# Two of the four token tiles of each late layer norm go to VectorE, the statistics' small sums too, and the queues behind the head loop are written in a new order

## The reference, cut to what matters

```python
x = x + attn_a(layernorm(x), ...)   # 16 heads of 64, causal softmax, output weights Wo, bo
x = x + ffn(layernorm(x), ...)      # 128 -> 512 -> 128, relu
x = x + attn_b(layernorm(x), ...)   # one head of 128, causal, a slope over the distance
x = x + ffn(layernorm(x), ...)      # the same weights again

def _layernorm(x, axis=-1, eps=1e-05):
    m = jnp.mean(x, axis=axis, keepdims=True)
    v = jnp.var(x, axis=axis, keepdims=True)
    return (x - m) / jnp.sqrt(v + eps)
```

## Time and profile before

| | |
|---|---|
| Median of 3 runs | 575.68 us (575.47 to 575.82) |
| Profiled execution, its own time | 579.0 us |
| Span in that profile | 577.0 us |
| Busy in the span | PE 528.2 us, ACT 468.5, POOL 455.8, DVE 444.7 |
| Slots | to about 417 us |
| Work behind the slots | about 417 to 577 us |

### The profile page before, as it was taken

How to read it: one execution, slowest core, us unless ns; L and a number is a source line. 1 busy time by engine, 2 the same in 40 slices (tenths; PEclk the granted TensorE clock), 3 DMA queues, 4 the chain that set the end, 5 groups by cost and what they waited for, 6 DMA issues and landing times.

```text
span 577.0 us, 17876 instructions
## 1 busy us (share of the span) xinstructions
PE 528.2 (92%) x6844; PEld 369.8 (64%) x6844; DVE 444.7 (77%) x1383; ACT 468.5 (81%) x923; POOL 455.8 (79%) x446
## 2 busy tenths in 40 slices
PE   4688999899999999999999999997988998788886
PEld 3445666566676667666766667664788795546664
DVE  5588888788888888888888888887776575689822
ACT  3659889889988999899989999889873869473983
POOL 5658899678888888888888888896965956564995
PEclk9989999999999999999999999999989999899999
DMA  9423334232433333423334243358108000000001
GB/s 230 113 56 72 85 86 111 56 94 58 119 84 94 93 76 102 104 74 96 80 104 110 56 121 77 100 141 319 39 38 292 2 3 2 1 1 2 1 20 55
DMA packets 36435, 48.54 MB, mean 84 GB/s; under 512 B 10728, under 2 KB 17792, under 8 KB 36352
## 3 DMA queue, kind: packets, MB, share of 16 engines
q1 hardware_dynamic: 34240, 46.88, 29.6%
q10 hardware_dynamic: 2112, 0.54, 0.4%
HBM read 12.79 MB, written 9.44 MB: 39 GB/s over the span
## 4 chain that ended last, share of the span: by engine, by line
PE 65%; ACT 10%; DVE 9%; issue 8%; POOL 7%; DMA 1%; POOLq 0%; ACTq 0%; DVEq 0%
PE psum L555 9%; PE psum L611 9%; PE psum L612 9%; PE psum L509 6%; PE psum L511 6%; PE psum L510 6%; PE psum L591 5%; PE psum L593 5%; PE psum L592 5%; PE psum L614 2%; ACT xn L1130 2%; ACT p_hl L1202 2%; POOL h_lo L2077 2%; POOL p_hlb L2084 2%; POOL p_hl L2004 2%
## 5 line engine op out<-in xcount | busy, mean ns | idle before, releaser
L2004 POOL TENSOR_TENSOR p_hl<-p,p_hl 128x512 f16<-128x512 f32 x288 | 327.4, 1162 | 54.0 <-ACT p_hl L1202 50.6
L1481 DVE CUSTOM_DVE_ANT_0 max_junk<-psum,mask_s 128x1024 bf16<-128x1024 f32 (+7 forms) x256 | 190.2, 753 | 32.0 <-issue 31.8
L1201 ACT ACTIVATE p<-psum 128x512 f32<-128x512 f32 x288 | 178.2, 619 | 16.4 <-PE psum L614 14.1
L1202 ACT ACTIVATE p_hl<-psum 128x512 f16<-128x512 f32 x288 | 179.6, 624 | 0.0
L591 PE MATMUL psum<-v_all,p_hl 128*128 128x65 f16 x1152 | 125.5, 193 | 1.7 <-POOL p_hl L2004 1.7
L611 PE MATMUL psum<-q_hl,k_hh 128*128 128x512 f16 (+3 forms) x384 | 125.1, 326 | 1.4 <-ACT p_hl L1202 1.4
L592 PE MATMUL psum<-v_all,p_hl 128*128 128x64 f16 x1152 | 125.6, 193 | 0.0
L593 PE MATMUL psum<-v_all,p_hl 128*128 128x65 f16 x1152 | 125.2, 194 | 0.0
L612 PE MATMUL psum<-q_hm,k_l 128*128 128x512 f16 (+3 forms) x384 | 121.8, 326 | 0.0
L591 PEld LDWEIGHTS psum<-v_all,p_hl 128*128 128x128 f16 x1152 | 107.4, 98 | 16.7 <-POOL p_hl L2004 1.8
L592 PEld LDWEIGHTS psum<-v_all,p_hl 128*128 128x128 f16 x1152 | 106.7, 97 | 4.9
(11 more groups left out here) (205 smaller groups left out, 1109.1 us busy)
## 6 DMA issues: line engine op xcount, KB each, us to landing
k_hh<-st_hi SPq DMA_DIRECT2D x64, 128.0 KB, 2.3
o_scratch<-o_sb SPq DMA_DIRECT2D x16, 512.0 KB, 2.6
o_in<-o_scratch SPq DMA_DIRECT2D x4, 2048.0 KB, 10.5
k_l<-st_lo SPq DMA_DIRECT2D x32, 128.0 KB, 2.3
q_hl<-st_hi SPq DMA_DIRECT2D x32, 128.0 KB, 2.3
q_hl<-st_lo SPq DMA_DIRECT2D x32, 128.0 KB, 2.3
q_hm<-st_hi SPq DMA_DIRECT2D x32, 128.0 KB, 2.3
x_sb<-in_L_attn_a_x SPq DMA_DIRECT2D x4, 256.0 KB, 3.7
```

The lines of the kernel that those rows point to most:

```text
L1201: nc.scalar.activation(p32[:, ring_at(u, r), :], src, ACT.Exp, scale=SCALE_A).then_inc(exp_done, 1)
L1202: nc.scalar.activation(p_hl[:, u % 2, 0, BANK * r:BANK * (r + 1)], src, ACT.Exp, scale=SCALE_A).then_inc(phi_done, 1)
L1481: nc.vector.tensor_tensor_reduce(out=max_junk[:, n % 2, 0:cols], in0=max_banks(v, j, 0, cols), in1=mask_s[:, S - cols:S], scale=1.0, scala ...
L2004: nc.gpsimd.tensor_tensor(p_hl[:, u % 2, 1, cols], p32[:, ring_at(u, r), :], p_hl[:, u % 2, 0, cols], ALU.subtract)\
```

## The change

Three things change.

1. `var_eps` and minus the mean are made by DVE at the end of `chunk_stats`, not by POOL. DVE first waits for its own `bn_aggr`. This holds for all chunks: 0 and 1 (`var_eps` alone), 2 and 3 in the slots, and the twelve behind them.
2. For the twelve chunks behind the slots ACT normalises two of the four tiles, and DVE the other two in a new step `norm_rest`, with the instruction that `chunk_norm` has. `turn_late` and `add_forward_row` wait for both.
3. The lists behind the slots stand in another order on PE, ACT, DVE and POOL.

```diff
@@ chunk_stats (DVE)
                 last.then_inc(aggr_done, 1)
+                dve.wait_ge(aggr_done, n + 1)
+                cols = slice(CT * c, CT * (c + 1))
+                nc.vector.tensor_scalar(var_eps[:, cols], mean_var[:, cols, 1], EPS, None, ALU.add).then_inc(eps_done, 1)
+                if n >= LATE_CHUNKS[0]:
+                    nc.vector.tensor_scalar(shift[:, cols], mean_var[:, cols, 0], -1.0, None, ALU.mult).then_inc(mean_turned, 1)
@@ new, DVE
+            def norm_rest(n):
+                dve.wait_ge(rstd_done, n + 1)
+                dve.wait_ge(xt_full, n - 1)
+                for j in range(CT // 2, CT):
+                    tile = CT * LN_ORDER[n][1] + j
+                    last = nc.vector.tensor_scalar(xn[:, n % 2, j, :], x_sb[:, tile, :], mean_var[:, tile, 0:1], rstd[:, tile:tile + 1],
+                                                   ALU.subtract, ALU.mult)
+                last.then_inc(xn_rest, 1)
@@ late_norm (ACT)
-                for j in range(CT):
+                for j in range(CT if n < CHUNKS else CT // 2):
@@ chunk_rstd, chunk_shift (POOL)
-                pool.wait_ge(aggr_done, n + 1)
-                nc.gpsimd.tensor_scalar(var_eps[:, cols], mean_var[:, cols, 1], EPS, None, ALU.add).then_inc(eps_done, 1)
...
-                nc.gpsimd.tensor_scalar(shift[:, cols], mean_var[:, cols, 0], -1.0, None, ALU.mult).then_inc(mean_turned, 1)
@@ turn_late (PE)
                 pe.wait_ge(xn_ready, n + 1)
+                pe.wait_ge(xn_rest, n - CHUNKS + 1)
@@ the list of DVE behind the slots, its head
             tail_norm()
-            tail_gain()
             outputs_out(HEADS - 2, 0)
             outputs_out(HEADS - 2, 1)
             block_low(0, 0)
             block_low(0, 1)
+            tail_gain()
             block_low(0, 2)
+            block_low(0, 3)
...
@@ the list of POOL, its end
             hidden_low(7, 2)
+            hidden_low(7, 3)
             add_forward_row(7)
-            hidden_low(7, 3)
```

More of the change, by code:

```diff
@@ L915, in outputs_b @@
                         last.then_inc(pvb_done, 1)
+            outputs(HEADS - 1, 0)
             turn_block(0, 0)
@@ L927, in _ @@
             turn_block(0, 6)
+            turn_block(0, 7)
             outputs(HEADS - 1, 3)
@@ L945, in _ @@
             turn_block(1, 7)
+            output_tile(0, 2)
             output_tile(0, 3)
@@ L979, in _ @@
             turn_block(3, 4)
+            forward(0, 2)
             turn_block(3, 5)
-            forward(0, 2)
             forward(0, 3)
@@ L1792, in _ @@
             block_low(0, 7)
+            outputs_out(HEADS - 1, 1)
             block_low(1, 0)
-            outputs_out(HEADS - 1, 1)
             block_low(1, 1)
             tail_low(1)
+            block_low(1, 2)
             tail_low(2)
-            block_low(1, 2)
-            add_result(0, 0)
-            tail_low(3)
             block_low(1, 3)
@@ L1803, in _ @@
             block_low(1, 5)
+            tail_low(3)
+            block_low(1, 6)
+            block_low(1, 7)
             tail_low(4)
-            block_low(1, 6)
+            add_result(0, 0)
             add_result(0, 1)
-            block_low(1, 7)
             late_stats(ln_of[1, 0])
             add_result(1, 0)
+            norm_rest(ln_of[1, 0])
             add_result(1, 1)
@@ L1815, in _ @@
             block_low(2, 2)
+            norm_rest(ln_of[1, 1])
             block_low(2, 3)
@@ L1826, in _ @@
             late_stats(ln_of[1, 2])
+            add_result(3, 0)
             block_low(3, 2)
[L1828 removed]
             block_low(3, 3)
             block_low(3, 4)
+            norm_rest(ln_of[1, 2])
+            add_result(3, 1)
             block_low(3, 5)
[L1832 removed]
+            block_low(3, 6)
             late_stats(ln_of[2, 0])
             add_result(4, 0)
[L1835 removed]
             block_low(3, 7)
             add_result(4, 1)
+            norm_rest(ln_of[2, 0])
             chunk_low(ln_of[1, 2])
             late_stats(ln_of[2, 1])
+            chunk_low(ln_of[2, 0])
+            norm_rest(ln_of[2, 1])
             add_result(5, 0)
[L1841 removed]
             add_result(5, 1)
@@ L1844, in _ @@
             queries_low(0)
+            norm_rest(ln_of[1, 3])
             chunk_low(ln_of[2, 1])
@@ L1867, in _ @@
             biased(0, 1)
+            norm_rest(ln_of[2, 3])
             biased(0, 2)
@@ L1918, in _ @@
             outputs_out_b(1, 7)
-            chunk_low(ln_of[3, 2])
+            norm_rest(ln_of[3, 2])
             add_result(8, 0)
             late_stats(ln_of[3, 3])
+            chunk_low(ln_of[3, 2])
+            norm_rest(ln_of[3, 3])
             add_result(8, 1)
+            add_result(9, 0)
             chunk_low(ln_of[3, 3])
-            add_result(9, 0)
             add_result(9, 1)
```

220 lines of the change are left out of this document (108 added, 112 removed).

## The result

The changed kernel takes 584.81 us (median of 6 runs, 583.81 to 586.91), the kernel before 576.81 beside it (6 runs, 575.47 to 579.67). The ratio is 1.0138, interval 1.0105 to 1.0171: 8.0 us longer. The two profiled executions differ by about the same, 586.91 against 579.0, and their spans by 7.9 (584.9 against 577.0), so the traces can be set against each other.

A forecast was written before the change was run, and what follows sets the result against it. PE was taken as the bound, busy 528.2 of 577.0 us. The terms 4.6 + 1.6 + 2.5 - 1.2 + 0.9 - 1.0 - 0.4 - 0.2 gave +6.8 on 575.68: 582.5 us, range 573.5 to 587.

The forecast's parts named there:

- Slower with 0.78: Whole kernel: chance 0.78 of being slower by more than 1.2 us; within that 0.08, faster 0.14.
- Slots u = 1 and 2, +4.6: Two slots with `chunk_stats`: sums ahead of `st_lo` wait for POOL, 2.3 us a slot, +4.6 us (0.6 to 4.8).
- the second to about 66.3: In the slot, the second small sum on DVE also waits for POOL, to about 66.3, so `st_lo` starts 2.3 us late.
- The clock behind it, +1.6: Behind these slots' longer PE stands of 2.6 us the clock falls: half of two falls, +1.6 us (0 to 3.2).
- `tail_gain`, +2.5 (0 to 5): Between second and third `block_low`: `tail_gain` waits for POOL and PE stands for the third block, +2.5 us.
- `output_tile(0, 2)`, -1.2: Behind chunk 1's last block: 1.3 us of PE work fills the stand of 1.18 at 438.96, -1.2 us.
- `norm_rest(1, 0)`, +0.9: Late norm of chunk (1, 0): `norm_rest` waits for POOL's `steps_sloped(0)`, +0.9 us (-1.2 to +2).
- `max_rows_b(0)`, -1.0: Before the second attention: moved ahead of `late_stats(2, 3)`, it takes statistics out of PE's stand of 2.02, -1.0 us.
- The second attention and the end, -0.4: DVE's extra sums and `norm_rest` +2.0 (0 to 4), against -1.2 for the last bias row and 1.2 at (3, 3).
- my two terms: At the end: -1.2 us from the last bias row leaving the last `h_lo`'s front, and 1.2 won at chunk (3, 3).
- The start, -0.2: At the kernel's start POOL's `rstd` begins without its own `var_eps`, -0.2 us.
- The rule and the row: Skill's port rule: four-column sums on DVE wait for POOL; by the one-column row `slope_g` they would not, slots 0.6 not 4.6.

The follow-up runs named there:

- b3: The kernel before with the small sums of chunks 2 and 3 on DVE, each written as four single columns: 579.44 us, ratio 1.0048.
- a2: The changed kernel with the small sums of chunks 0 to 3 made on POOL again: 580.02 us, ratio 1.0047.
- b2: The kernel before with only the small sums of chunks 2 and 3 on DVE, four columns wide: 579.86 us, ratio 1.0034.
- a5: The changed kernel with `tail_gain` and `tail_root` back in their early places and the first four chunks' sums on POOL: 577.38 us, ratio 1.0000.
- a1: The changed kernel with `tail_gain` alone back behind `tail_norm`: 582.58 us, ratio 1.0101.
- b4: The kernel before with `max_rows_b(0)` ahead of `late_stats(2, 3)` and the last bias row behind the last low hidden part: 577.87 us, ratio 1.0027.
- a7: a5 with all four tiles of each late norm on ACT and `norm_rest` left out: 581.48 us, ratio 1.0085.
- a4: The changed kernel with `tail_root` early, `tail_gain` left where the change has it, first four chunks' sums on POOL: 583.99 us, ratio 1.0117.
- a6: The changed kernel in its own order, with the small sums and `tail_gain` as single columns: 581.4 us, ratio 1.0092.
- c1: a5 with `tail_gain` in single columns: 579.57 us, ratio 1.0047.

## Why the prediction was right

Slower with 0.78, and the median of 584.81 lies in the range of 573.5 to 587, 2.3 above the forecast; 1.1 of that is the kernel before, at 576.81 beside it where 575.68 stood. By differences it was +6.8 against +8.0. That the sum comes so near is luck: the terms for the slots and the clock behind them were 3.7 us too large, and the first slot (+1.5, no term for it), the stretch to the first `h_hi` (+3.75 against +2.2) and what lies behind it (0 against -1.4) make up for it. Two stretches of 3.4 us more at the lower clock are in the 7.9 us between the two profiles; at 1.6 us each, by b3, they are some 3 of them (an estimate). At the same clock, 0.985, the changed kernel's runs took 583.8 and 585.0 us and those of before 578.6 to 580.4.

*Slots u = 1 and 2, +4.6.* Right place and mechanism, half the size: +2.46 (a2 and b2 show it alone). The step that failed is "the second to about 66.3": I let each of two instructions in a row wait for one of POOL's, as in `tail_gain`. The second took 0.15 to 0.16 us in every run with this form.

*The clock behind it, +1.6.* Nothing. PE stood 1.47 us and not 2.6, and no window behind it shows a lower clock. The lower clock came elsewhere, in the first slot, by +1.5, which I had no term for.

*`tail_gain`, +2.5 (0 to 5).* Too small. From a2 to a5, which differ by the places of `tail_root` and `tail_gain`, the stretch from the last `q_hm` to the first `h_hi` falls from 43.80 to 40.45, and from the changed kernel 4.4: so 3.4 to 4.4 us, the lower clock behind the stand (6.8 us, in a5 none) included. Against the kernel before the whole stretch grew by 3.75. I read PE's stand and its half clock rightly and missed the other half of the place: with `tail_root` late on POOL, putting `tail_gain` back is worth nothing (a1). "DVE reaches it at about 420.2" was wrong too; it came at 424.49, since DVE stood 5.04 us for PE in front of `outputs_out`.

*`output_tile(0, 2)`, -1.2, and `norm_rest(1, 0)`, +0.9.* The stand of 1.18 is gone as forecast. `norm_rest(1, 0)` took its plain 0.60 us, since DVE got in 0.4 us ahead of POOL's slope step. What a5 is ahead of before over this stretch, 0.66 us, is no gain of theirs: before has 3.4 us at the lower clock there and a5 none, and against b3, which has none either, a5 is 1.0 us behind. In a5 one tile of `norm_rest(1, 0)` did wait, 1.14 us.

*`max_rows_b(0)`, -1.0.* The stand went from 2.02 to 1.64, -0.4. b4 shows where such a gain goes when the statistics come later: into a stand for `xT_lo`.

*The second attention and the end, -0.4.* The end came out about as forecast: the stand for the last `h_lo` is gone, and behind the last exponential the kernel takes 1.92 us less, against the 2.4 of my two terms. Ahead of it, from the first `h_hi` on, it takes 1.95 more at the same length of lower clock, where my +2.0 and -1.0 (`max_rows_b`) gave +1.0; four `norm_rest` (of (3, 0) to (3, 2), and (2, 3) ahead of them) are blocked for 1.4 to 2.1 us. What I left out is that the new order stands on the split (a7: about 4 us by the timed runs, 1.76 of them outside of the clock).

*The start, -0.2.* +0.43 in one profile against one, and the first `q_hm` lay between 35.3 and 38.3 in the others: nothing can be read from it.

*The rule and the row.* The Trainium skill, SBUF — State Buffer, section Who interferes with whom, says that a `tensor_scalar` in its mode with two ports and POOL exclude each other for whole instructions. The traces agree for four and five columns (1.16 us against 0.16 to 0.17 where POOL is idle); the wait for a whole run in a4 is more than that. A single column of the same operation isn't held: 0.14 to 0.15 us each beside a busy POOL (b3). Which form waits set the size of the loss and not its sign: a6, with single columns, is still slower than before.

## What to carry to other kernels

A small SBUF-to-SBUF operation on VectorE beside a busy GpSimd can cost whatever GpSimd is in the middle of (1.1 us here), and that can be the rest of its run (5.8). Look for what is queued behind it before you put it in front of a critical instruction; written as single columns it didn't wait here, though the wait went on to the next wide instruction. When an operation is moved, move its producer on the other engine with it, and undo both when it is tested: half an undo moved the stand and left its length.

## What the runs showed of the hardware that I had not expected

A wide instruction on VectorE may wait for one instruction of GpSimd or for a whole run: 1.07 to 1.20 us each in `tail_gain` of before, 5.80 us in a4; and `wo_lo`, 128x1024, took 2.45 (a5), 3.50 (a6) and 3.79 us (c1) against 1.27 beside an idle GpSimd, and ended each time 1.1 us behind GpSimd's run. Of two equal instructions in a row the second can take 0.16 us where the first took 1.16. `tensor_tensor` of a single column waits (1.06 us), the same product as `tensor_scalar` doesn't (0.21).

The time of an execution goes with its mean granted clock. Among the 24 runs of the kernel before in the second set, it was 574.9 us at 0.997, 574.5 at 0.996, 575.6 to 576.3 at 0.993 and 0.994, 577.2 to 578.4 at 0.988, 579.1 and 580.4 at 0.985. The times of one kernel lay up to 5.9 us apart. Differences of 2 us between versions have to be read from stretches of the traces, or from many runs.
